# Hi/lo splits moved across a step boundary, in V's phase and at the last step, and x of the next step loaded a third of a step later

## The reference, cut to what matters

```python
q, k, v = proj(x, Wq), proj(x, Wk), proj(x, Wv)
q = q * minimum(cond, 4.0)
scores = where(causal, q @ k.T / sqrt(64), finfo.min)
y = (softmax(scores) @ v).reshape(b, s, 1024) @ Wo.T
q_w = clip(round(w / mean(abs(w))), -1, 1) * mean(abs(w))
q_x = clip(round(y / scale), -128, 127) * scale      # scale = max(abs(y), axis=-1) / 127
return x + q_x @ q_w.T + bias
```

## Time and profile before

| | us |
|---|---|
| median of 3 runs | 2084.48 |
| lowest and highest | 2084.17, 2085.92 |
| the profiled execution | 2085.09 |
| its span, first to last instruction | 2083.3 |
| TensorE busy (matmuls) | 1991.5 (96%) |
| VectorE busy | 1416.1 (68%) |
| ScalarE busy | 1114.4 (53%) |
| GpSimd busy | 888.4 (43%) |
| TensorE's mean granted clock | 0.994 |

### The profile page before, as it was taken

One profiled execution on the slowest core, in us unless ns is written; L12 is line 12 of the kernel. 1 busy time (PEld: TensorE's weight loads), 2 busy tenths in 40 slices (PEclk: granted clock), 3 DMA queues, 4 the chain that ended last, 5 costly groups with the idle time before them and its releaser, 6 DMA issues.

```text
span 2083.3 us, 34749 instructions
## 1 busy us (share of the span) xinstructions
PE 1991.5 (96%) x10074; PEld 1617.8 (78%) x10074; DVE 1416.1 (68%) x3277; ACT 1114.4 (53%) x2497; POOL 888.4 (43%) x816
## 2 busy tenths in 40 slices
PE   8999998999999999999999999999997999999998
PEld 6877886788788788787788787787886777777775
DVE  6667774777778777778777778777777554545454
ACT  4554444777767677768777778777775000000000
POOL 0343332544444444444444445444444544444442
PEclk9999999999999999999999999999999999999999
DMA  6666555333453443453433443433443423232322
GB/s 206 222 220 210 200 176 181 122 125 101 146 156 102 135 128 101 144 159 102 147 116 106 151 151 103 151 110 111 146 147 96 146 91 121 91 121 91 121 91 81
DMA packets 200981, 282.43 MB, mean 136 GB/s; under 512 B 11216, under 2 KB 146384, under 8 KB 199760
## 3 DMA queue, kind: packets, MB, share of 16 engines
q1 hardware_dynamic: 200384, 281.07, 42.8%
q10 hardware_dynamic: 528, 0.52, 0.1%
HBM read 178.79 MB, written 69.21 MB: 119 GB/s over the span
## 4 chain that ended last, share of the span: by engine, by line
PE 72%; DVE 10%; issue 6%; ACT 6%; DMA 3%; POOL 1%; DVEq 0%; SPq 0%; ACTq 0%; POOLq 0%
PE proj_ps L174 24%; PE proj_ps L509 8%; PE s_ps L509 8%; PE o_ps L317 6%; PE o_ps L580 5%; PE t_ps L870 5%; PE t_ps L283 5%; PE o_ps L870 3%; PE s_ps L243 2%; PE s_ps L242 2%; DVE q_st L219 2%; ACT parts L359 2%; DVE prob L254 2%; DVE parts L365 1%; ACT prob L261 1%
## 5 line engine op out<-in xcount | busy, mean ns | idle before, releaser
L174 PE MATMUL proj_ps<-parts 128*128 128x512 f32 x3072 | 840.9, 408 | 0.0
L273 POOL TENSOR_TENSOR prob<-prob,row_inv 128x128 f32<-128x128 f32 (+3 forms) x512 | 387.6, 757 | 696.2 <-DVE row_inv L267 691.2
L174 PEld LDWEIGHTS proj_ps<-parts 128*128 128x128 f32 x3072 | 540.6, 190 | 95.8
L261 ACT ACTIVATE prob<-prob,row_min 128x128 f32<-128x128 f32 (+3 forms) x512 | 287.7, 562 | 176.7 <-DVE row_min L254 171.4
L254 DVE CUSTOM_DVE_ANT_0 prob<-s_ps,mask 128x128 f32<-128x128 f32 (+3 forms) x512 | 248.2, 485 | 58.5 <-PE s_ps L243 25.2
L283 PE MATMUL t_ps<-ident,prob 128*128 128x128 f32 x1280 | 228.2, 277 | 53.1 <-DVE pt_lo L304 50.8
L297 ACT ACTIVATE pt_hi<-t_ps 128x128 fp32r<-128x128 f32 (+3 forms) x512 | 220.1, 430 | 107.6 <-PE t_ps L283 104.5
L565 ACT ACTIVATE yt_q<-t_ps 128x1024 bf16<-128x1024 bf16 x32 | 32.7, 1023 | 427.1 <-PE t_ps L558 427.1
L304 DVE TENSOR_TENSOR pt_lo<-t_ps,pt_hi 128x128 fp32r<-128x128 f32 (+3 forms) x512 | 249.1, 487 | 17.7 <-ACT pt_hi L297 12.1
L283 PEld LDWEIGHTS t_ps<-ident,prob 128*128 128x128 f32 x1280 | 152.4, 141 | 77.8 <-DVE pt_lo L304 44.5
L365 POOL TENSOR_TENSOR parts<-x_raw,parts 128x512 fp32r<-128x512 f32 x128 | 192.3, 1503 | 17.7 <-ACT parts L359 17.7
(11 more groups left out here) (118 smaller groups left out, 2891.3 us busy)
## 6 DMA issues: line engine op xcount, KB each, us to landing
x_raw<-xT SPq DMA_DIRECT2D x128, 512.0 KB, 5.5
v_scratch<-v_out SPq DMA_DIRECT2D x64, 512.0 KB, 3.3
k_sw<-k_st SPq DMA_DIRECT2D x128, 256.0 KB, 3.7
v_st<-v_scratch SPq DMA_DIRECT2D x128, 256.0 KB, 2.7
oT_scratch<-o_sum SPq DMA_DIRECT2D x64, 256.0 KB, 2.1
x_raw<-oT_scratch SPq DMA_DIRECT2D x32, 512.0 KB, 4.7
x_tile<-x SPq DMA_DIRECT2D x32, 512.0 KB, 5.3
out<-res SPq DMA_DIRECT2D x32, 512.0 KB, 3.2
```

The lines of the kernel that those rows point to most:

```text
L174: mm = pe.matmul(out, l, r, start=(k == 0 and i == 0), stop=(k == KT - 1 and i == 2))
L261: act.activation(prob[:, u % 4, 0:w], prob[:, u % 4, 0:w], ACT.Exp, bias=row_min[:, u % 4:u % 4 + 1], scale=-1.0, accum_out=row_sum[:, u % ...
L273: pool.tensor_tensor(prob[:, u % 4, 0:w], prob[:, u % 4, 0:w], row_inv[:, u % 4:u % 4 + 1].broadcast_to([P, w]), ALU.mult).then_inc(norm_d ...
```

## The change

It reorders work on each engine and changes no arithmetic.

- Boundary, ScalarE: H(2) ahead of evac_hi(3); x_high(4) and x_high(5) from the end of a step to behind evac_hi(3) of the next.
- Boundary, VectorE: L(2) ahead of evac_lo(3) and batch_scale; x_low(4) from the end of a step to behind M(6) of the next. GpSimd: x_low(5) from behind normalise(4) to ahead of normalise(5).
- SyncE: load_x from behind swap_k(1) to behind swap_k(0) and load_v(0); in the first step to behind swap_k(0), the wait for all stores of V, load_v(0) and load_v(1).
- V's phase: wf_abs(2(n - 3)) from the end of pair n to behind v_copy A and the split of B11, wf_abs(2(n - 3) + 1) to behind the split of T3; wf_add_partitions two products later; wf_scale and the three parts of wf_ternary later; in the last pair x_high(4..7) behind v_copy R.
- End: o_high(0) and o_high(1), o_low(0) and o_low(1) from the ending step into the last step before it; o_high of these tiles no longer waits for x_free.

```diff
@@ o_high
             if isinstance(t, int) and t < 2:
-                eng.wait_ge(x_free, STEPS * KT)
                 eng.activation(o_hi[p], o_raw[p], ACT.Copy).then_inc(o_hi_done, 1)
@@ v_pe
                 v_product(pe, n, A11)
+                v_product(pe, n, S4)
+                v_product(pe, n, A12)
                 if n == WF_FROM:
                     wf_add_partitions(pe)
-                v_product(pe, n, S4)
-                v_product(pe, n, A12)
@@ v_act
                 v_copy(act, n, V_TMP_A)
                 xv_split(act, n + 1, B11, False)
+                wf_abs(act, 2 * (n - WF_ABS_FROM))
...
                 if n == PAIRS - 1:
-                    for k in range(KT):
+                    for k in range(4):
                         x_high(act, 0, k)
                 xv_split(act, n + 1, T2, False)
                 v_copy(act, n, V_TMP_R)
+                if n == PAIRS - 1:
+                    for k in range(4, KT):
+                        x_high(act, 0, k)
                 xv_split(act, n + 1, T1, False)
                 xv_split(act, n + 1, T3, False)
+                wf_abs(act, 2 * (n - WF_ABS_FROM) + 1)
...
                 v_high(act, n, 3)
-                if WF_ABS_FROM <= n < WF_ABS_FROM + KT // 2:
-                    for k in range(2):
-                        wf_abs(act, 2 * (n - WF_ABS_FROM) + k)
@@ v_dve
                 xv_split(dve, n + 1, B22, True)
-                if n == WF_FROM:
-                    wf_scale(dve)
-                wf_ternary(dve, n - WF_FROM, 0)
...
                 v_low(dve, n, 0)
-                wf_ternary(dve, n - WF_FROM, 1)
                 xv_split(dve, n + 1, T2, True)
+                if n == WF_FROM:
+                    wf_scale(dve)
+                wf_ternary(dve, n - WF_FROM, 0)
...
                 xv_split(dve, n + 1, T1, True)
-                wf_ternary(dve, n - WF_FROM, 2)
                 v_sum(dve, n, 1)
                 v_sum(dve, n, 2)
                 xv_split(dve, n + 1, T3, True)
+                wf_ternary(dve, n - WF_FROM, 1)
...
                 xv_split(dve, n + 1, T4, True)
+                wf_ternary(dve, n - WF_FROM, 2)
                 v_low(dve, n, 3)
@@ act_step
+            H(2)
             if old:
                 evac_hi(act, o, 3)
-            if ending:
-                o_high(act, 0, 0)
-            H(2)
             WO(2)
+            if now and old:
+                x_high(act, n, 4)
+                x_high(act, n, 5)
             E(5)
             if now and old:
                 x_high(act, n, 6)
@@ act_step, late in the step
             E(10)
-            if ending:
-                o_high(act, 1, 1)
...
             X(0, 1)
             if last and now:
+                o_high(act, 0, 0)
                 wo_high(act, 0)
...
             OL(3)
-            X(4, 5)
+            if last and now:
+                o_high(act, 1, 1)
@@ dve_step
+            L(2)
             if old:
                 evac_lo(dve, o, 3)
                 if now:
                     batch_scale(dve, n, now[2])
-            L(2)
             I(5)
             M(6)
             if now and old:
+                x_low(dve, n, 4)
                 x_low(dve, n, 6)
...
             M(5)
-            X(4)
@@ pool_step
-            if ending:
-                o_low_part(pool, 0, 0)
+            if now and old:
+                x_low(pool, n, 5)
             for u in range(5, UNITS):
                 if old:
                     normalise(pool, o, u)
...
-                    if nxt and 2 <= u:
+                    if nxt and 2 <= u < 4:
                         x_low(pool, x, 2 * u - 3)
+                    if last and u == 3:
+                        o_low_part(pool, 0, 0)
+                if last:
+                    o_low_part(pool, 1, 1)
@@ sp_step
                 swap_k(sp, old[0], 1)
-            if nxt:
-                load_x(sp, *nxt)
...
             if now:
                 swap_k(sp, now[0], 0)
             if now and old:
+                if nxt:
+                    load_x(sp, *nxt)
                 load_v(sp, *now, 1)
```

More of the change, by code:

```diff
@@ L934, in wf_abs @@
         def wf_abs(act, k):
+            if not 0 <= k < KT:
+                return
             act.wait_ge(wf_in[k % 2], (k // 2 + 1) * 16)
@@ L1523, in pool_step @@
                     x_low(pool, n, 7)
-                if u == 10 and ending:
-                    o_low_part(pool, 1, 1)
             if ending:
```

## The result

The changed kernel took 2134.45 us (median of 4, 2127.56 to 2139.18), the kernel before 2085.2 us beside it: a ratio of 1.0232 (95%: 1.0198 to 1.0266). The forecast was 2085 us, its range 2075 to 2094. The profiled execution after took 2137.94 us, its span is 2136.2 us (before 2083.3), its mean granted clock 0.975 (before 0.994).

A forecast was written before the change was run, and what follows sets the result against it. TensorE is busy nearly throughout, so time could come only from its waits or clock. Boundary +4, weight-loading steps -1, first step with A22 -11, V's phase +8.4, end 0: +0.4 us, giving 2085 us, range 2075 to 2094.

The forecast's parts named there:

- the visible wait at T(4) hides the swap's: Step boundaries: with T(4)'s 1.4 us wait gone, TensorE would wait about as long at S(8) for k_sw's swap.
- the boundary without the clock: The 31 step boundaries: L(3) and T(5) slightly later, +0.05 to +0.3 us at 25 of them; sum +4 us.
- Rival 3: Step boundaries: L(3) becomes the step's bound at 0.5 us a step, +12 instead of +4, 2093 us; chance 0.17.
- the clock at the boundary, charged at nothing: The 31 step boundaries: their sum of +4 us held no term for a lower clock behind the waits.
- V's phase: Pairs 3 to 6: early wf_abs delays S1, +9.1 us, less 3.4 at wf_add_partitions, plus 2.7 for the clock: +8.4 us.
- x later and A22: First step and end of V's phase: no wait before S(0), -4.85, its clock -3.0, shorter A22 -3.1: -11 us.
- The other term of x: Steps that also load weights: k_sw(0) no longer queues behind x, a 1.1 us wait at 624 us goes: -1 us.
- The end: Last steps: YY(0) starts 1.2 us earlier, T(5) then waits for H(3): sum 0 us (-2 to +2).

The follow-up runs named there:

- e5: Kernel before, with the second half of k_sw's swap issued between load_v(2) and load_v(3) of the step that makes it: 2083.88 us.
- e10: Kernel before, with only H(2) moved ahead of evac_hi(3) and L(2) ahead of evac_lo(3): 2092.47 us.
- e6: Changed kernel, with the second half of k_sw's swap issued between load_v(2) and load_v(3) of the step that makes it: 2134.5 us.
- e2: Kernel before, with only the change's edits of V's phase: 2093.82 us.
- e3: Kernel before, with only load_x moved behind swap_k(0), in the first step behind two load_v too: 2080.97 us.
- e4: Kernel before, with only the change's edits of the last two steps (o_high and o_low a step forward): 2087.75 us.
- e13: Changed kernel, with both wf_abs of a pair back at the pair's end on ScalarE: 2117.35 us.
- e1: Kernel before, with only the change's boundary edit, load_x left where it was: 2135.26 us.
- e9: Kernel before, with x_low(5) of the next step on VectorE behind x_low(4), no longer on GpSimd: 2131.01 us.
- e12: Kernel before, with k_sw's swap issued early, T(4) behind J(0,2,3) and T(5) behind J(0,4) on TensorE, and load_x behind swap_k(0): 2058.75 us.
- e15: Kernel e12, with x_high(4) to (7) behind v_copy R at the end of V's phase: 2052.41 us.
- e7: Changed kernel, with x_low(4) and x_low(6) behind L(3) on VectorE: 2123.37 us.
- e8: Changed kernel, with k_sw's swap issued early and x_low(4) and x_low(6) behind L(3) on VectorE: 2119.07 us.
- the early swap: Second half of k_sw's swap issued between load_v(2) and load_v(3) of the step that makes it; alone in the kernel before (e5): 2083.88 us.
- e14: Changed kernel, with k_sw's swap issued early, x_low(6) behind L(3) on VectorE, and x_high(6) and x_high(7) behind H(3) on ScalarE: 2065.03 us.

## Why the prediction was wrong, step by step

- **Right: the visible wait at T(4) hides the swap's.** S(8) now waits for the landing in 30 steps (46.7 us), T(5) for L(3). e5, e10 and e6 show the three deadlines one by one.
- **Mis-sized: the boundary without the clock.** The forecast was 0.1 to 0.2 us a step (steps of 38.6 to 38.8), measured was 0.5 (39.0 where the clock held). VectorE's timeline of the changed kernel, o_add(3), M(6), x_low(4) and (6), L(3), against the earlier trace rows:

```profile
1174.69 0.68 DVE L334 TENSOR_TENSOR o_sum<-o_ps,o_low 64x512 f32<-64x512 f32 x1 [0.46 <-ACT o_low L326]
...
1178.70 0.56 DVE L254 CUSTOM_DVE_ANT_0 prob<-s_ps,mask 128x384 f32<-128x384 f32 x1
...
1179.18 1.71 DVE L365 TENSOR_TENSOR parts<-x_raw,parts 128x512 fp32r<-128x512 f32 x2
1180.81 0.68 DVE L304 TENSOR_TENSOR pt_lo<-t_ps,pt_hi 128x512 fp32r<-128x512 f32 x1
```

  From o_add(3)'s start to L(3)'s end it is 6.80 us, where 6.63 was forecast and 6.33 stood before. Most of the rest are handovers: 0.08 us more ahead of M(6), 0.09 from M(6) to L(3), 0.08 before T(5). Rival 3 (0.5 us a step, 12 us) named this size.
- **The step that failed: the clock at the boundary, charged at nothing.** The sum priced the new standstill by its length alone. It has no term for the clock there and gives no reason for that; it charges the clock only in the first step, at A22 and in V's phase. That the standstill grew from 1.4 to 1.9 us was in the forecast's own mechanism (0.5 us a step was even priced, as a rival); that each such step could pay 1.6 us more for its clock was not. 22 steps of 1.6 us are 35 us, the larger part of the miss. The trace before held a warning: the longest of its boundary waits, the 2.6 us at 720 us, was the only one behind which the clock fell. It was a faint one: the same wait lost the clock in e2 and e3 too, but kept it in e4 and e5.
- **V's phase: mechanism right, clock under-sized.** The waits before S1 were forecast as 2 to 4 us each, 9.1 us together once two small waits before S2 were taken off; measured were 3.99, 2.88, 2.66 and 2.07 us, 11.6 together. The clock was charged at two waits of four, 2.7 us; it fell at all four. By e13 wf_abs forward costs 18.2 us: 11.6 of waits, which leaves 6.6 for the clock. Two of four was charged because the clock had stayed at 1.00 through one wait of 3.4 us. That was luck of one trace: in all nine other runs that leave wf_abs and wf_add_partitions in their old places (e1, e3 to e5, e9 to e12, e15) the clock fell behind the same wait of 3.0 to 3.5 us. TensorE's timeline of e3, and the stretch behind it:

```profile
158.13 0.60 PE L942 MATMUL s_ps<-wf_sums,ones 128*128 128x8 f32 x2 [3.44 <-ACT x_raw L936]
```

```profile
158.00:161.00 3.00, 2.87 (x8) 0.50 1.07 294
```

  The Trainium skill (TensorE: Matmul & The Clock Gate, What's actually happening) says that the gate goes by how busy TensorE has been of late. The prediction gave that rule half weight. The changed kernel's trace agrees with it in four waits of four (e2, e6, e7 and e8, with the same waits, in three of four).
- **Right: x later and A22.** Forecast -11 us, measured -12.2 in the first step; A22 kept 0.31 us of its wait, where 1.3 was forecast. In the whole kernel load_x alone gave -6.2. The other term of x, -1 us for a wait at 624 us, did not come: in e3 that wait is gone, but one of 1.08 us for pt_lo stands later in the same step, and the step is 0.2 us shorter.
- **The end: 0 forecast, +3.8 measured.** The o parts moved forward cost nothing (e4). By e1 it would be the boundary's order, by e13 not; this stays open.

Together: forecast 4 - 1 - 11 + 8.4 + 0; measured about +48 for the steps with load_x's share in them, -12 in the first step, +13 in V's phase, +4 at the end.

## What to carry to other kernels

Price a growing standstill of TensorE twice: by its length, and by the chance that the clock is granted at half behind it, times the steps; here 0.5 us more a step cost 1.6 us more in 22 steps of 30. That the wait of today keeps the clock says nothing of one half a microsecond longer; look what the clock did behind the longest waits of the trace, and in more than one execution: a clock that held once, as at the wait of 3.4 us here, is no evidence. And where three deadlines stand behind each other, fill the wait with work that needs none of them (TensorE's next products: -24 us together with the early swap, which alone gave -2) rather than bring them forward one by one (-2 to +48 us).

## What the runs showed of the hardware

- A wait of 1.9 to 2.0 us before otherwise gapless work brought the clock to 1.2 GHz in 21 or 22 steps of 30 (e1, e6, e9), whether in one piece or two and at either place. One of 1.51 to 1.66 us at S(8) did so in no step (e10), nor one of 1.72 to 1.75 us at T(4) (15 cases, before and e2 to e5), nor one of 0.86 us (e14); but 1.51 us in two pieces did so in 17 steps (e8). With equal waits a step either loses 1.3 to 1.6 us or nothing: the steps of the changed kernel with a standstill of 1.9 us took 39.0 or 40.5 to 40.9 us, none between.
- A wait of 3.0 to 3.5 us in V's phase lost the clock in nine executions and kept it in one (wf_add_partitions, one trace for each run).
- Two x_low behind each other took VectorE 1.71 us, 0.86 each, while GpSimd was at work too; before, x_low(4) took 0.92 and x_low(6) 0.86. So the second one brought no contention of its own.
